# Every third half-tile of the factor layer multiplied in fp32, directly from the ring

## What is computed

```python
c = layernorm(cond) * ln_gamma + ln_beta
h = gelu(c @ W1 + bias1)                       # 16 x 512
w = h @ W2 + bias2                             # 16 x 16384: the factor layer
a1, b1, a2, b2 = [t.reshape(16, 512, 8) for t in split(w, 4)]
mid = gelu(x @ base_down + (x @ a2) @ b2.T)    # per sequence
x = x + x + mid @ base_up.T + (mid @ b1) @ a1.T
xW = x @ Wx + b
h_t = tanh(xW_t + h_(t-1) @ Wh)                # 512 steps, one after the other; h_0 = cond
y = x + hs
```

## Time and profile before

| | us |
|---|---|
| median of 3 runs | 1421.26 |
| lowest, highest | 1417.79, 1422.94 |
| the profiled execution, its own time | 1420.18 |
| its span in the profile | 1418.2 |
| TensorE, VectorE, ScalarE busy | 1320.6, 971.4, 690.9 |
| factor layer, first rounding to last remainder | 14.8 to 165.4 |

### The profile page before, as it was taken

One profiled execution on the slowest core, in us unless ns is written; L12 is line 12 of the kernel. 1 busy time (PEld: TensorE's weight loads), 2 busy tenths in 40 slices (PEclk: granted clock), 3 DMA queues, 4 the chain that ended last, 5 costly groups with the idle time before them and its releaser, 6 DMA issues.

```text
span 1418.2 us, 49800 instructions
## 1 busy us (share of the span) xinstructions
PE 1320.6 (93%) x20524; PEld 1069.6 (75%) x20524; DVE 971.4 (68%) x3757; ACT 690.9 (49%) x2483; POOL 241.0 (17%) x525
## 2 busy tenths in 40 slices
PE   6677799999999999999999999999999999999996
PEld 3333488878887888787888888787888788878864
DVE  5577665777677767776767777777767776767564
ACT  4565435454545544545445454545454545454442
POOL 0100011121121112121212121212111121212111
PEclk9787799999999999999999999999999999999998
DMA  9577601030211111211112120202121212101011
GB/s 320 186 240 206 204 5 29 4 51 11 41 23 32 32 32 32 33 32 32 32 30 34 20 45 9 48 10 47 17 37 27 32 32 32 32 2 32 3 32 31
DMA packets 292273, 75.66 MB, mean 53 GB/s; under 512 B 273072, under 2 KB 273088, under 8 KB 292048
## 3 DMA queue, kind: packets, MB, share of 16 engines
q1 hardware_dynamic: 292048, 72.49, 23.1%
HBM read 55.68 MB, written 16.78 MB: 51 GB/s over the span
## 4 chain that ended last, share of the span: by engine, by line
PE 79%; DVE 8%; ACT 5%; issue 3%; DMA 3%; SPq 0%; DVEq 0%; ACTq 0%; POOLq 0%; POOL 0%
PE bulk L851 40%; PE rec L872 27%; PE bulk L840 7%; PE bulk L854 4%; DMA work<-in_L_cond_W_dram 3%; ACT hf L485 2%; DVE act_s L606 2%; DVE act_s L691 2%; PE bulk L823 2%; DVE z L665 1%; DVE mid_s L606 1%; ACT rec L472 1%; ACT act_s L494 1%; DVE hs L673 1%; DVE hs L670 0%
## 5 line engine op out<-in xcount | busy, mean ns | idle before, releaser
L872 PEld LDWEIGHTS rec<-hs,wh_s 128*128 128x128 f16 x16352 | 444.9, 96 | 141.1 <-DVE hs L673 111.0
L485 ACT ACTIVATE hf<-z,scl 128x32 f32<-128x32 f32 x1024 | 273.4, 314 | 556.2 <-DVE z L665 552.0
L872 PE MATMUL rec<-hs,wh_s 128*128 128x32 f16 x16352 | 497.5, 177 | 22.9 <-ACT rec L472 17.9
L665 DVE TENSOR_REDUCE z<-rec 128x32 f32<-128x96 f32 x1024 | 230.3, 256 | 195.5 <-PE rec L872 186.4
L415 POOL TENSOR_TENSOR work<-work,hf 128x64 f32<-128x64 f32 x352 | 156.3, 444 | 691.6 <-DVE hs L673 691.6
L670 DVE TENSOR_SCALAR hs<-hf 128x32 f16<-128x32 f32 x1024 | 181.9, 178 | 100.6 <-ACT hf L485 100.5
L673 DVE SCALAR_TENSOR_TENSOR hs<-hf,hs 128x32 f16<-128x32 f32 x1024 | 197.0, 192 | 35.3
L851 PE MATMUL bulk<-act_s,down_s 128*128 128x512 f32 x768 | 217.9, 407 | 0.0
L851 PE MATMUL bulk<-mid_s,up_s 128*128 128x512 f32 x768 | 215.6, 407 | 0.0
L851 PE MATMUL bulk<-act_s,wx_s 128*128 128x512 f32 x768 | 203.4, 404 | 0.0
L472 ACT ACTIVATE rec<-work 128x32 f32<-128x32 f32 x1008 | 181.6, 210 | 0.0
(11 more groups left out here) (126 smaller groups left out, 1088.4 us busy)
## 6 DMA issues: line engine op xcount, KB each, us to landing
work<-in_L_cond_W_dram SPq DMA_DIRECT2D x33, 1024.0 KB, 5.6
work<-in_x_dram SPq DMA_DIRECT2D x256, 64.0 KB, 3.6
out_dram<-work SPq DMA_DIRECT2D x256, 64.0 KB, 2.3
stage<-in_L_cond_base_up_dram SPq DMA_DIRECT2D x1, 1024.0 KB, 17.4
stage<-in_L_cond_base_down_dram SPq DMA_DIRECT2D x1, 1024.0 KB, 11.8
stage<-in_L_cond_Wx_dram SPq DMA_DIRECT2D x1, 1024.0 KB, 14.4
stage<-in_L_cond_Wh_dram SPq DMA_DIRECT2D x1, 1024.0 KB, 13.9
bias2T<-in_L_cond_bias_dram SPq DMA_DIRECT2D x4, 16.0 KB, 3.6
```

What stands on the lines that cost most here:

```text
L485: nc.scalar.activation(hf[:, t % 4, half], z[:, half], ACT.Tanh, scale=inv).then_inc(tanh_done, 1)
L665: nc.vector.tensor_reduce(z[:, f * HT:(f + 1) * HT], R[f].rearrange("p m j b -> p m b j"), AX.X, ALU.add).then_inc(z_done, 1)
L872: last = nc.tensor.matmul(R[fo][:, m, 0:PARTS, :], wh_s[:, q, k, n * P:(n + 1) * P], hs[:, k, :, :], start=(m == k == q == 0), stop=(k == ...
```

## The change

`SPLIT` is the list of the half-tiles with n % 3 != 2, 22 of 32. The other ten (n = 2, 5, ..., 29) are neither rounded nor given a remainder. TensorE waits for their load itself and multiplies them with four fp32 matmuls that read the ring slot; the 32 stationary columns are the unrounded h of 16 sequences and 16 columns of zeros (`hT` has grown by these). The ring slot of such a half-tile is free when its matmuls are done (`row_mm`), no longer when its remainder is made. `w2_s` is used by the number i of a half-tile within `SPLIT`, i % 2, and the semaphores `w2_hi`, `w2_lo`, `row_hi` count these alone. Since `SPLIT[i + 2]` is n + 3 for both kinds of split half-tile, ScalarE rounds n + 3 in step n.

```diff
--- before.py
+++ after.py
@@ -167,7 +167,7 @@
         vecs = work[0:4 * KT, 5, 2 * D:2 * D + P]
         ln = sb("ln", [B, 8])
         cT = sb("cT", [P, KT, B])
-        hT = sb("hT", [P, KT, B])
+        hT = sb("hT", [P, KT, 2, B])
         h_s = sb("h_s", [P, KT, 2, B], F32R)
         fsum = sb("fsum", [P, RANK, B])
         vT = sb("vT", [P, 4, KT])
@@ -250,6 +250,13 @@
         xw_placed = sem("xw_placed")
         sum_done = sem("sum_done")
 
+        SPLIT = [n for n in range(HALVES) if n % 3 != 2]
+
+
+        def split_no(n):
+
+            return SPLIT.index(n)
+
         w2_v = w2.rearrange("(k p) n -> p k n", p=P)
 
         W2_TILES = [(q, dt) for q in (2, 3, 1, 0) for dt in range(KT)]
@@ -331,8 +338,10 @@
 
             def load_w2(n):
                 q, dt = W2_TILES[n // 2]
-                if n >= RING:
-                    sp.wait_ge(w2_lo, n - RING + 1)
+                if n >= RING and n - RING in SPLIT:
+                    sp.wait_ge(w2_lo, split_no(n - RING) + 1)
+                elif n >= RING:
+                    sp.wait_ge(row_mm, n - RING + 1)
                 c0 = q * QUARTER + dt * W2C + n % 2 * 512
                 sp.dma_start(work[:, n % RING, :].rearrange("p (k n) -> p k n", k=KT),
                              w2_v[:, :, c0:c0 + 512]).then_inc(w2_in[n % RING], 16)
@@ -425,11 +434,12 @@
 
             def w2_high(n):
 
+                i = split_no(n)
                 act.wait_ge(w2_in[n % RING], 16 * (n // RING + 1))
-                if n >= 2:
-                    act.wait_ge(row_hi, n - 1)
-                    act.wait_ge(w2_lo, n - 1)
-                nc.scalar.copy(w2_s[n % 2][:, HI].rearrange("p k n -> p (k n)"), work[:, n % RING, :]).then_inc(w2_hi, 1)
+                if i >= 2:
+                    act.wait_ge(row_hi, i - 1)
+                    act.wait_ge(w2_lo, i - 1)
+                nc.scalar.copy(w2_s[i % 2][:, HI].rearrange("p k n -> p (k n)"), work[:, n % RING, :]).then_inc(w2_hi, 1)
 
             w2_high(0)
 
@@ -437,7 +447,7 @@
             act.wait_ge(vT_done, 1)
             for m in range(KT):
                 h1 = bulk[:, 1, m * B:(m + 1) * B]
-                nc.scalar.activation(hT[:, m, :], h1, ACT.Gelu, bias=vT[:, 2, m:m + 1])
+                nc.scalar.activation(hT[:, m, 0, :], h1, ACT.Gelu, bias=vT[:, 2, m:m + 1])
                 last = nc.scalar.activation(h_s[:, m, HI, :], h1, ACT.Gelu, bias=vT[:, 2, m:m + 1])
             last.then_inc(hT_done, 1)
             w2_high(1)
@@ -451,8 +461,8 @@
                 nc.scalar.copy(dst[:, HI], src).then_inc(fac_hi, 1)
 
             for n in range(HALVES):
-                if n + 2 < HALVES:
-                    w2_high(n + 2)
+                if n in SPLIT and split_no(n) + 2 < len(SPLIT):
+                    w2_high(SPLIT[split_no(n) + 2])
                 if RING < n <= RING + KT:
                     act.wait_ge(up_tr, n - RING)
                     nc.scalar.copy(up_s[:, HI, n - RING - 1], bulk[:, 4 + (n - RING - 1) % 2, :]).then_inc(up_hi, 1)
@@ -579,6 +589,7 @@
                                                vT[:, 1, k:k + 1], ALU.mult, ALU.add)
             last.then_inc(cT_done, 1)
             h0 = bulk[:, 0, KT * B:2 * KT * B].rearrange("p (k b) -> p k b", k=KT)
+            nc.vector.memset(hT[:, :, 1, :], 0.0)
             nc.vector.memset(h0s[:], 0.0)
             nc.vector.memset(ones[:], 1.0)
             nc.vector.memset(sc1[:], 0.0)
@@ -599,10 +610,11 @@
 
             def w2_low(n):
 
-                dve.wait_ge(w2_hi, n + 1)
-                if n >= 2:
-                    dve.wait_ge(row_mm, n - 1)
-                dst = w2_s[n % 2].rearrange("p s k n -> p s (k n)")
+                i = split_no(n)
+                dve.wait_ge(w2_hi, i + 1)
+                if i >= 2:
+                    dve.wait_ge(row_mm, SPLIT[i - 2] + 1)
+                dst = w2_s[i % 2].rearrange("p s k n -> p s (k n)")
                 nc.vector.tensor_tensor(dst[:, LO], work[:, n % RING, :], dst[:, HI].bitcast(F32),
                                         ALU.subtract).then_inc(w2_lo, 1)
 
@@ -638,11 +650,12 @@
 
             w2_low(0)
             dve.wait_ge(hT_done, 1)
-            nc.vector.tensor_tensor(h_s[:, :, LO, :], hT[:], h_s[:, :, HI, :].bitcast(F32),
+            nc.vector.tensor_tensor(h_s[:, :, LO, :], hT[:, :, 0, :], h_s[:, :, HI, :].bitcast(F32),
                                     ALU.subtract).then_inc(h_split, 1)
 
             for n in range(1, HALVES):
-                w2_low(n)
+                if n in SPLIT:
+                    w2_low(n)
                 if RING < n <= RING + KT:
                     split_up(n - RING - 1)
                 if n >= 4 and n % 2 == 0:
@@ -815,13 +828,22 @@
 
             pe.wait_ge(h_split, 1)
             for n in range(HALVES):
-                for part, ready, done in ((HI, w2_hi, row_hi), (LO, w2_lo, row_mm)):
-                    pe.wait_ge(ready, n + 1)
+                if n not in SPLIT:
+                    pe.wait_ge(w2_in[n % RING], 16 * (n // RING + 1))
+                    pe.wait_ge(row_done, n - 1)
+                    for k in range(KT):
+                        last = nc.tensor.matmul(bulk[0:2 * B, 2 + n % 2, :], hT[:, k].rearrange("p s b -> p (s b)"),
+                                                work[:, n % RING, k * 512:(k + 1) * 512], start=(k == 0),
+                                                stop=(k == KT - 1))
+                    last.then_inc(row_mm, 1)
+                for part, ready, done in ((HI, w2_hi, row_hi), (LO, w2_lo, row_mm)) if n in SPLIT else ():
+                    i = split_no(n)
+                    pe.wait_ge(ready, i + 1)
                     if part == HI and n >= 2:
                         pe.wait_ge(row_done, n - 1)
                     for k in range(KT):
                         last = nc.tensor.matmul(bulk[0:2 * B, 2 + n % 2, :], h_s[:, k].rearrange("p s b -> p (s b)"),
-                                                w2_s[n % 2][:, part, k, :], start=(part == HI and k == 0),
+                                                w2_s[i % 2][:, part, k, :], start=(part == HI and k == 0),
                                                 stop=(part == LO and k == KT - 1))
                     last.then_inc(done, 1)
                 if n >= 3 and n % 2:
```

## The result

| | us |
|---|---|
| changed kernel, median of 4 runs | 1449.37 (1446.97 to 1449.66) |
| kernel before, median of 4 runs | 1421.04 (1417.79 to 1422.94) |
| ratio | 1.0198, 95% interval 1.0176 to 1.0220 |
| changed kernel, profiled execution | 1449.4, span 1447.7 |
| last remainder of the factor layer ends, before | 165.4 |

The account below looks back on a forecast made before the run. The prediction took a loop over two engines, VectorE and ScalarE, to bound the factor layer. +8 us at 2.4 GHz and +8 for the clock, total +16 on the profiled 1420.2, gave 1437 us, range 1423 to 1452.

Parts of the forecast that it names:

- The loop: Factor layer, end of D through its slot's reload and ScalarE's rounding to next D: 26.8 to 27.3 us per six half-tiles.
- D: Four fp32 matmuls of a direct half-tile on TensorE: 3.6 us at 2.4 GHz, 7.0 at 1.2.
- The rival of one cycle a column: Factor layer: an fp32 record costs one cycle a column, D 2.25 us at 2.4 GHz; 1418 to 1423 us, chance 0.12.
- that of five: Factor layer: fp32 records cost 5 cycles a column, D 8.5 us; 1476 us, chance 0.03.
- The sum: Factor layer worked through at 2.4 GHz, last remainder ending at 173.5 instead of 165.4: +8.1 us; the clock added +8.
- The D's, 7.2 forecast: Clock term: eight D's on the path at the mean grant of 0.79 are longer, 7.2 us in all.
- The matmuls ahead of D(8), D(11), D(17) and D(23), 0.8 forecast: Clock term: remainder matmuls standing ahead of three D's on the path take 0.8 us more.
- The loads from D(8) to D(23), 0 forecast: Reload of the slot D frees, 5.6 us from the end of D to ScalarE's rounding; nothing added.
- The cold rival: Factor layer: D's fall mostly in cold stretches that feed themselves, +30 to +38, 1451 to 1459 us; chance 0.11.
- the D's would hold the clock at 2.4 GHz: Rival, factor layer: TensorE stays at 2.4 GHz, +8, 1429 us; chance 0.22.
- the ring wait is hidden: Rival, factor layer: the shorter two-engine loop shows, 22 us for six half-tiles, 1414 us; chance 0.04.
- Costs taken at nothing: The memset of hT (0.2 us if idle time were gone), its strided write, and SyncE's new wait, priced at nothing.

Follow-up runs that it names:

- Experiments 2: The changed kernel with a fifth ring slot, in the buffer of Wh: 1412.1 us, ratio to the kernel before 0.9944.
- 3: The kernel before with the same fifth ring slot, as control: 1415.9 us, ratio 0.9972.
- 12: The kernel before, with the slots of n % 3 == 2 released when their matmuls are done, not when their remainder is made: 1420.6 us, ratio 1.0003.
- experiment 1: The changed kernel with only the first two of four row blocks multiplied in each direct product: 1427.5 us, ratio to the kernel before 1.0048.
- Experiment 6: The changed kernel with 72, 24 and 8 added matmuls, none before remainder matmuls from n = 24 on or before D(29): 1438.3 us.
- experiments 4 to 6: The changed kernel with added matmuls where TensorE idles: 1445.9 us; with more of them: 1445.2 us; the same but none at the end: 1438.3 us.
- experiment 11: The kernel before with five ring slots and the x loads issued one at a time behind the loads of n = 12 to 27: 1413.3 us.

## Why the prediction was right, and where it was off

**The direction and the mechanism** hold. The loop runs as written, D(8) to D(23) alternating between 17.4 to 18.7 and 15.1 to 15.4 us where 15.05 to 15.6 and 11.7 were worked out for the full clock. Experiments 2, 3 and 12 show the cause: one more slot takes the loss away, helps the kernel before by only 5 us, and the release without D costs nothing. The size was less well met: 12 us too small, near the upper end of the range.

**D** was priced at two cycles a column, 3.6 us at 2.4 GHz. It is 3.6: D(2) and D(5) ran wholly at that clock.

```profile
26.32 3.59 PE L835 MATMUL bulk<-work,hT 128*32 128x512 f32 x8 [0.85 <-ACT work L474]
40.17 3.59 PE L835 MATMUL bulk<-work,hT 128*32 128x512 f32 x8 [3.04 <-ACT work L474]
```

Four records take 1.88 us (experiment 1) and eight 3.59, so a record takes 0.43 us, what an fp32r record of the earlier trace rows takes at 1.2 GHz. The rival of one cycle a column falls, and so does that of five: at two cycles, 32 columns are 0.03 of the 0.12 us that a record of L867 took the earlier trace rows, so most of it was not columns, which the comparison with the transposition had missed. The four passes of the Trainium skill ("FP8 and Floating Point Precision", TensorE Precision Notes) agree with it: two records of two passes.

**The sum** was too small by 12 us. In the profiled executions the spans differ by 29.5 us, where the sum had 8.1 at the full clock and 8 for the clock. L(31) ends at 192.6 and not at the 173.5 worked out for the full clock. The timeline of the changed kernel divides these 19.1 us as follows, and 2.3 come behind them:
- The D's, 7.2 forecast: 11.1. The eight of the path took 39.9 us together instead of 28.8 at 2.4 GHz. The mis-sized step is the use of the mean grant of the kernel before, 0.79. The mean grant after is 0.77, nearly what was assumed; but the low stretches fall on the D's. D(8) to D(23) took 4.8, 4.5, 6.4, 4.7, 6.4 and 5.3 us, on average 5.4 and not 4.5, and over D(14) and D(20) the grant was 0.56. TensorE had idled for 2.2 and 2.3 us just before these two, and for 6.9 to 7.5 us before the remainder matmuls ahead of the other four. Idle time does not always bring the low clock: D(5) came behind 3.0 us of it and was granted 1.00. The reader should price a matmul that comes after a wait by the clock it finds there, not by the mean.
- The matmuls ahead of D(8), D(11), D(17) and D(23), 0.8 forecast: 3.4. Four remainder matmuls that took 1.9 us instead of 1.1 are most of it.
- The loads from D(8) to D(23), 0 forecast: 3.8. I had taken 5.6 us from the end of D to H; the five took 6.1 to 6.8. In the changed kernel the issues of several loads wait behind D and go out within a few us, and the median from issue to landing is no longer 5.5 (62 to 160 us; no run tests whether the bunching is the reason):

```profile
work<-in_L_cond_W_dram SPq DMA_DIRECT2D x16, 1024.0 KB, 6.6
```

- Smaller latencies on the way to L(31), 0.8.
- Behind L(31), 0 forecast: 2.3 us. The first 13.4 us there were granted 0.75 after and 0.83 before:

```profile
192.60:206.00 13.40, 11.92 (x63) 10.48 (x64) 9.96 (x25) 5.21 (x8) 0.13 (x1) 0.75 0.51 81
...
165.40:178.80 13.40, 12.24 (x66) 10.29 (x66) 10.07 (x26) 5.21 (x8) 0.61 (x1) 0.83 0.51 80
```

  That the clock is the whole cause of the 2.3 us is argued, not shown.

Experiment 6 checks the clock's part: with the grant at 0.98 L(31) ends at 180.2, 12.4 us earlier, though its added matmuls stood in the way of D's for 4.8 us. The loads there still took 29.9 us in five instead of 28.0, so part of their term is not the clock's.

**The rivals.** The cold rival (D's mostly in cold stretches that feed themselves, 1451 to 1459, 0.11) is nearer to the measured 1449.4 than the forecast of 1437, and its mechanism is part of what ran: idle time, a low clock on most of the D's, a later load. The forecast had the loop right and this share too low; that the time still fell inside the range is in part luck, since half of this rival was inside it. That the D's would hold the clock at 2.4 GHz did not come: the mean fell slightly. The statement of the Trainium skill ("TensorE: Matmul & The Clock Gate", What's actually happening) that activity releases the throttle agrees with experiments 4 to 6, where added matmuls raised the grant from 0.77 to 0.89, 0.93 and 0.98; what was wrong was my reading of which way this kernel would go. That the ring wait is hidden was given 0.04 and 1414 us; with five slots, where most of it is hidden, the time was 1412.1 and six half-tiles took 23 to 24 us where 22 were priced. The price of that case was near, and the kernel was not in it.

**Costs taken at nothing.** The memset of hT and its strided write show nowhere: the first fp32r matmuls started at 19.0, before at 19.3. The path from D(23) to H(28) was 21.3 us for 20.9. One reading was off without effect: in the earlier trace rows the clock is below 9 tenths in the second to fifth digit and in the last.

## What to carry to other kernels

When a buffer is released by a later or longer step than before, the question is not how much later on average but when its next use is wanted: follow one slot around the ring, from the end of the new reader through the load to the step that stands behind it in the in-order queues. Removing work from the engines gained nothing here while the loop ran through a load, and one more buffer turned the same change from a loss of 2% into a gain of 0.3% (0.6% with what the buffer gains by itself). Where TensorE works in bursts after waits, a wait can be paid twice, once as such and once as the lower clock of the burst behind it.

## What the runs showed of the hardware that was not expected

- Added matmuls, 6 to 72 of 128 columns, most of them in TensorE's idle time, made the kernel 9 to 11 us faster.
- In the changed kernel, where loads go out in bunches, they landed 6.6 us after their issue in the median instead of 5.5, though the DMA share fell from 0.74 to 0.57 (65.6 to 142.1 us). That the bunches are the reason is not tested.
- An fp32 matmul of 512 columns is two records of 0.43 us each at 2.4 GHz, two cycles a column in each.
- The loads of x, 64 KB each in packets under 512 B, delay the 1 MB loads of W2 issued beside them: with four in a row H(24) and H(18) waited 5.4 and 4.8 us, with one in a row 4.2 and 3.8, and with none beside them they did not wait for a load. In the kernel before with one in a row (experiment 11) no rounding behind n = 7 waited for a load.
